# Attention beside scan: decays in SBUF, turned states in two banks, and a new order on four engines

## The chip, the cores and the metric

One core of a Trainium2 chip runs the kernel. The metric is the device time of one execution in microseconds; the time of a kernel is the median of its runs.

## The reference, cut to what matters

Four batches (B = 4) of 512 rows of 512 values pass through two blocks. The first is a selective scan over the context, gated by the normalised rows; the second is causal attention with 16 heads, followed by a mixture of experts.

```python
# first block, for every batch: u is 512 channels x 512 steps, state 512 x 16
dA = exp(delta[..., None] * A)
state = state * dA + (delta * u)[..., None] * B_t
y_t = einsum('ben,bn->be', state, C_t)
...
x = x + tanh(g_xattn) * (y + D * u) * silu(layernorm(x))
# second block
scores = q @ k * HEAD_DIM ** -0.5, causal
ctx = softmax(scores) @ v
h = rms(x + ctx @ wo)
x = x + tanh(g_ffn) * (attention and experts of h)
```

## The kernel before, in words

Everything is float32 (TensorE's large products are split in a high and a low part). Each engine runs its own list of instructions, written out by hand; semaphores are the only link between the lists, and an engine's order is fixed by the order of its calls. Rounds of all engines run as `round_(b, s)` with s = b + 1: the attention of batch b beside the scan of batch s. Ahead of them `first_scan` does batch 0's scan alone, and the fourth round has attention only, with the first pieces of the experts. The experts' part, `moe_stage`, comes last.

In a round, preparations come first (input projection of the context `cT`, convolution, delta, the products for q, k and v). Then `units(b, s)` runs: 16 quads (NQ = 16) of four heads of one block of 128 query rows (T4 = 4 blocks; in block i the scores are 128 x 128(i+1) wide), beside 64 scans (NB = 64: 16 states n times 4 channel blocks et). This is the stage that the change is about; it occurs three times, with s = 1, 2 and 3. Its pieces:

- scan k: ScalarE writes the decay exp(DL * aneg), 128x512, into `decay_bank(s, k)` (line 1269); GpSimd multiplies GB = DU * BB into a ring of four (line 2281, it waits for the scan four before, for its place); VectorE scans both into HS (line 1770), which is a ring of two states n.
- state q: TensorE turns a block of HS into `state_bank(s, q)` (line 705), VectorE adds it, weighted with C, into YA (line 1781).
- attention: TensorE computes the scores of a quad (lines 762 and 765), VectorE the row maxima (line 1826), ScalarE the exponentials EX (`probs`, line 1306), TensorE turns them into the one bank PB (line 775), ScalarE copies them to PT (`keep_turned`, line 1314), TensorE weighs V (`weigh`, lines 786 and 790), ScalarE copies the turned inverse (line 1319), VectorE makes the context cn (line 1836), ScalarE and GpSimd its high and low part (lines 1325 and 2324). VectorE's `invert` (line 1831) and GpSimd's `widen` (line 2318) make the inverse row sums.
- `finish(b, i, step)`: steps of a finished block of rows (output product, residual XL, its gated sum into xa on line 1846, RMS norm, router), spread over the quads of the next block.

SP issues the transfers in its own list: one row of B for each n (`load_b_row`), the rows that finish, and the context of the next batch but one (`load_ctx`). After the stage VectorE ends the scan's output, and TensorE, once the output product of the last rows is done, makes the input projection of the next batch from cT (line 647), on which ScalarE starts the convolution (line 1209).

PSUM has eight banks: A[0] to A[3] hold the scores, CX the context, PB the turned probabilities, HT0 and HT1 are the last two. In the three stages before the change all decays go through HT1 and all turned states but the last three through HT0:

```python
return (A[0], A[2], A[3])[q - (NB - 3)] if q >= NB - 3 else HT0   # state_bank, s > 0
return (HT0, A[0])[q % 2]                                          # state_bank, s == 0
return (HT1, A[1])[k % 2] if s == 0 else HT1                       # decay_bank
if k > (s == 0): act.wait_ge(scan_done, NB * s + k - (s == 0))     # before a decay
if s and 0 < q < NB - 3: pe.wait_ge(y_acc, adds(s, q))             # before a state is turned
```

Elsewhere VectorE has instructions of the same 128x512 with both operands in SBUF: the gate `z_gate` on line 1741 (in the first scan it reads PT and ZS, in later rounds GB and ZS), and the sum into xa on line 1846. Line 1340 is a ScalarE instruction from SBUF to SBUF with a scale for each partition.

## Time and profile before

| | |
|---|---|
| median of 3 runs | 1789.75 us (1787.08 to 1792.86) |
| the profiled execution | 1790.59 us |
| its span in the profile | 1788.8 us |
| TensorE, share of the span | 84% |
| VectorE | 65% |
| ScalarE | 51% |
| GpSimd | 45% |
| mean granted TensorE clock | 0.902 of full speed |
| the three stages, first scan to last | 234.6 to 395.7, 481.7 to 644.8, 730.8 to 890.8 us |

Busy shares are of the whole span, which holds stages of very different kinds: scan, attention beside scan, attention alone, experts. A share says little about any one of them; the rows below are cut by stage where that matters. Times of the profile are microseconds from the start of the span.

### The profile page before, as it was taken

To read this page: it belongs to the slowest core of one execution; us is meant where nothing else is said; L and a number is where in the kernel's file an instruction comes from. 1 tells how busy PE (TensorE), PEld (TensorE's weight loads), DVE (VectorE), ACT (ScalarE), POOL (GpSimd) and SP (SyncE) were. 2 spreads that over 40 slices of the span, in tenths; PEclk is the share of its full clock that TensorE was granted. 3 is DMA by queue.
4 is the path that set the end of the run, shared out by engine and by line. 5 is a ranking of instruction groups with operands and counts; after the bars stand their busy time and mean duration, and the time that the engine had idled before them with its cause. 6 is when DMAs were issued, how large, how long until landed. Compare 5 with 4: busy or idle time off the path is not lost.

```text
span 1788.8 us, 26797 instructions
## 1 busy us (share of the span) xinstructions
PE 1503.7 (84%) x9168; PEld 1150.6 (64%) x9168; DVE 1166.9 (65%) x1699; ACT 916.2 (51%) x2038; POOL 810.2 (45%) x807
## 2 busy tenths in 40 slices
PE   5677967788777789677878998799999999999994
PEld 2344645565445556455655666688787999999973
DVE  5987589996699985899945444432324666566545
ACT  5675457764467753567724663221213666666510
POOL 1992266542466532565413211243422555555444
PEclk8789968899878899788988999899999999999997
DMA  4460001111011111011132004721311877777464
GB/s 168 153 229 19 25 23 55 54 43 54 7 35 55 54 36 31 19 47 54 37 123 95 30 32 160 293 77 59 110 37 65 307 243 253 261 241 253 155 221 165
DMA packets 94664, 195.76 MB, mean 109 GB/s; under 512 B 8945, under 2 KB 25841, under 8 KB 91201
## 3 DMA queue, kind: packets, MB, share of 16 engines
q1 hardware_dynamic: 89408, 177.26, 29.1%
q0 software_dynamic: 5120, 16.78, 2.8%
q8 instruction: 75, 1.23, 0.3%
q14 instruction: 61, 0.49, 0.1%
HBM read 140.40 MB, written 53.61 MB: 108 GB/s over the span
## 4 chain that ended last, share of the span: by engine, by line
PE 55%; DVE 16%; issue 15%; POOL 7%; ACT 5%; DMA 1%; SPq 1%; DVEq 0%; ACTq 0%; POOLq 0%
PE scores L631 21%; PE bank L631 14%; DVE HS L1770 6%; DVE YA L1781 4%; PE bank L705 3%; PE bank L775 3%; POOL GB L2281 2%; PE bank L790 2%; ACT bank L1269 2%; PE bank L825 2%; PE scores L762 2%; POOL yab L2471 2%; PE scores L749 1%; PE bank L1092 1%; PE scores L765 1%
## 5 line engine op out<-in xcount | busy, mean ns | idle before, releaser
L2281 POOL TENSOR_TENSOR GB<-DU,BB 128x512 f32<-128x512 f32 x256 | 326.8, 1298 | 36.1 <-DVE DL L1752 21.2
L1770 DVE TENSOR_TENSOR_SCAN HS<-bank,GB 128x512 f32<-128x512 f32 x224 | 272.0, 1214 | 20.3 <-ACT bank L1269 17.6
L705 PE MATMUL bank<-ident,HS 128*128 128x128 f32 x860 | 165.8, 325 | 120.9 <-DVE YA L1781 104.9
L705 PEld LDWEIGHTS bank<-ident,HS 128*128 128x128 f32 x860 | 115.2, 165 | 166.3 <-DVE YA L1781 129.8
L1269 ACT ACTIVATE bank<-DL,aneg 128x512 f32<-128x512 f32 x224 | 154.7, 691 | 110.0 <-DVE HS L1770 108.2
L775 PE MATMUL bank<-ident,EX 128*128 128x128 f32 x640 | 131.5, 306 | 34.2 <-ACT PT L1314 20.9
L631 PE MATMUL scores<-xth,wgh 128*128 128x256 f32 x552 | 158.1, 286 | 2.2 <-DVE fa L2162 1.3
L1781 DVE SCALAR_TENSOR_TENSOR YA<-bank,Ct,YA 128x512 f32<-128x512 f32 x199 | 147.0, 738 | 14.2 <-PE bank L705 12.8
L631 PE MATMUL scores<-xth,wgl 128*128 128x256 f32 x552 | 156.1, 283 | 0.0
L631 PE MATMUL scores<-xtl,wgh 128*128 128x256 f32 x552 | 156.1, 283 | 0.0
L1314 ACT ACTIVATE PT<-bank 128x128 f32<-128x128 f32 (+3 forms) x256 | 110.3, 431 | 72.0 <-PE bank L775 64.9
L1306 ACT ACTIVATE EX<-scores,nm 128x128 f32<-128x128 f32 (+3 forms) x256 | 132.3, 521 | 22.4 <-DVE nm L1826 21.7
L775 PEld LDWEIGHTS bank<-ident,EX 128*128 128x128 f32 x640 | 79.8, 154 | 75.0 <-issue 47.0
L2426 POOL TENSOR_TENSOR wgl<-wgr,wgh 128x768 fp32r<-128x768 f32 x54 | 110.9, 2057 | 30.4 <-ACT wgh L1580 30.4
L2443 POOL TENSOR_TENSOR fal<-fa,fah 128x512 fp32r<-128x512 f32 x30 | 38.8, 1293 | 162.7 <-ACT fah L1609 162.5
L2324 POOL TENSOR_TENSOR ctl<-cn,cth 128x128 fp32r<-128x128 f32 x64 | 29.3, 458 | 180.7 <-ACT cth L1325 180.7
L631 PEld LDWEIGHTS scores<-xth,wgh 128*128 128x128 f32 x552 | 105.7, 191 | 3.6 <-DVE fa L2162 1.7
L631 PE MATMUL scores<-hah,wgh 128*128 128x512 f32 x272 | 106.7, 392 | 1.0 <-issue 1.0
L631 PE MATMUL scores<-hal,wgh 128*128 128x512 f32 x272 | 106.5, 391 | 0.0
L631 PE MATMUL scores<-hah,wgl 128*128 128x512 f32 x272 | 106.3, 391 | 0.0
L631 PEld LDWEIGHTS scores<-xtl,wgh 128*128 128x128 f32 x552 | 105.7, 192 | 0.9
L631 PEld LDWEIGHTS scores<-xth,wgl 128*128 128x128 f32 x552 | 105.7, 191 | 0.0
(294 smaller groups left out, 3798.6 us busy)
## 6 DMA issues: line engine op xcount, KB each, us to landing
wgr<-wffn_in SPq DMA_DIRECT2D x108, 384.0 KB, 6.5
wdr<-wffn_in SPq DMA_DIRECT2D x81, 256.0 KB, 3.1
BB<-b_scratch SPq DMA_DIRECT2D x64, 256.0 KB, 3.3
xr<-xg SPq DMA_DIRECT2D x23, 512.0 KB, 5.8
yg<-ysb SPq DMA_DIRECT2D x23, 512.0 KB, 6.5
xg<-V SPq DMA_DIRECT2D x11, 1024.0 KB, 5.8
hah<-hhd SPq DMA_DIRECT2D x5, 1024.0 KB, 14.1
hal<-hhd SPq DMA_DIRECT2D x5, 1024.0 KB, 16.1
```

Source lines behind the costliest of these rows:

```text
L631: mm = nc.tensor.matmul(out_, parts[a](k), rhs_parts[b](k), start=(k == 0 and j == 0), stop=(k == n - 1 and j == 2))
L705: mm = nc.tensor.transpose(state_bank(s, q)[:, et * P:(et + 1) * P], HS[:, n % 2, et, tt * P:(tt + 1) * P], ident[:])
L762: nc.tensor.matmul(SB[:, a, 0:W], QK[r:r + HD, m, i * P:(i + 1) * P], QK[r:r + HD, 4 + m, 0:W], start=True, stop=False)
L775: mm = nc.tensor.transpose(turned_bank(b, v)[:, kb * P:(kb + 1) * P], EX[:, a, kb * P:(kb + 1) * P], ident[:])
L1269: nc.scalar.activation(decay_bank(s, k), DL[:, et, :], ACT.Exp, scale=aneg[:, et, n:n + 1]).then_inc(dA_ready, 1)
L1306: nc.scalar.activation(EX[:, a, 0:W], SB[:, a, 0:W], ACT.Exp, bias=nm[:, a:a + 1], accum_out=rs[:, q % 2, a:a + 1]).then_inc(ex_done, 1)
L1314: nc.scalar.activation(PT[:, a, 0:W], turned_bank(b, v)[:, 0:W], ACT.Copy).then_inc(pt_done, 1)
L1770: nc.vector.tensor_tensor_scan(HS[:, n % 2, et, :], decay_bank(s, k), GB[:, k % 4, :], 0.0, ALU.mult, ALU.add).then_inc(scan_done, 1)
L1781: nc.vector.scalar_tensor_tensor(YA[:, tt, :], state_bank(s, q), Ct[:, tt, n:n + 1], YA[:, tt, :], ALU.mult, ALU.add).then_inc(y_acc, 1)
L2281: nc.gpsimd.tensor_tensor(GB[:, k % 4, :], DU[:, et, :], BB[:, n % 2, :], ALU.mult).then_inc(gb_ready, 1)
L2426: nc.gpsimd.tensor_tensor(wgl[raw][:, c, :], wgr[raw][:, c * 2 * EW:(c + 1) * 2 * EW], wgh[raw][:, c, :].bitcast(f32), ALU.subtract).then_ ...
L2443: nc.gpsimd.tensor_tensor(fal[:, b % 2, c, :], fa[:, s % 2, :], fah[:, b % 2, c, :].bitcast(f32), ALU.subtract).then_inc(f_al, 1)
```

## The change

Decays of the three stages move from the PSUM bank HT1 to two halves of cT, the context's place in SBUF, which lies idle once the input projection has read it. A decay waits for the scan two before, not one. Turned states use HT0 and HT1 in turn, and one is turned once the state two before has been added. As the decays now lie in cT, the next context is loaded after the stage's last scan and not ahead of the stage. The order of the instructions in `units` is written anew on TensorE, ScalarE, VectorE and GpSimd; the instructions themselves, their sizes and their number stay as they are.

```diff
@@ -380,7 +380,7 @@
 
             if s == 0:
                 return (HT0, A[0])[q % 2]
-            return (A[0], A[2], A[3])[q - (NB - 3)] if q >= NB - 3 else HT0
+            return (A[0], A[2], A[3])[q - (NB - 3)] if q >= NB - 3 else HT[q % 2]
 
         def z_bank(s, tt):
 
@@ -406,7 +406,8 @@
             return VT * NS + NB * (s - 1) + q
 
         def decay_bank(s, k):
-            return (HT1, A[1])[k % 2] if s == 0 else HT1
+
+            return cT[:, k % 2, :] if s else (HT1, A[1])[k % 2]
 
         def turned_bank(b, v):
 
@@ -430,6 +431,8 @@
         def _(sp):
             def load_ctx(s):
                 at(sp, xp_mm, T4 * s)
+                if s > 1:
+                    sp.wait_ge(scan_done, NB * s)
                 sp.dma_start(cT[:], ctx_in[s]).then_inc(ctx_in_s, 16)
 
             def load_x(s, i):
@@ -502,8 +505,6 @@
                 if s < B:
                     sp.wait_ge(xd_ready, s + 1)
                     sp.dma_start(b_scratch[s], xd[DR:DR + NS, :]).then_inc(b_stored, 16)
-                    if 0 < s < B - 1:
-                        load_ctx(s + 1)
                     sp.wait_ge(b_stored, 16 * (s + 1))
                     for n in range(2):
                         load_b_row(s, n)
@@ -537,6 +538,8 @@
                     i, m = quad(q)
                     if b >= 0 and i and m:
                         rows_out(b, i - 1, m - 1)
+                if 0 < s < B - 1:
+                    load_ctx(s + 1)
 
             begin()
             for r in range(-1, B):
@@ -699,8 +702,8 @@
                         pe.wait_ge(y_acc, adds(0, q - 1))
                     else:
                         pe.wait_ge(kept, 2 * weighed(m, ut) + 2)
-                if s and 0 < q < NB - 3:
-                    pe.wait_ge(y_acc, adds(s, q))
+                if s and 1 < q < NB - 3:
+                    pe.wait_ge(y_acc, adds(s, q - 1))
                 for et in range(T4):
                     mm = nc.tensor.transpose(state_bank(s, q)[:, et * P:(et + 1) * P],
                                              HS[:, n % 2, et, tt * P:(tt + 1) * P], ident[:])
@@ -887,20 +890,14 @@
                 for q in range(-2, NQ + 1):
                     now, next_, last = 0 <= q < NQ, 0 <= q + 1 < NQ, 0 < q
                     i, m = quad(q)
-                    row = i - 1 if now and i else None
-                    if now:
-                        turn(b, HG * q + 1)
-                    if last:
-                        turn_states(s, T4 * (q - 1) + 1)
                     if now:
                         turn(b, HG * q + 2)
-                    if row is not None and m != 1:
-                        finish(b, row, (0, None, 1, 2)[m])
-                    if last:
-                        turn_states(s, T4 * (q - 1) + 2)
+                    if now and i and m != 1:
+                        finish(b, i - 1, (0, None, 1, 2)[m])
                     if now:
                         turn(b, HG * q + 3)
                     if last:
+                        turn_states(s, T4 * (q - 1) + 2)
                         turn_states(s, T4 * (q - 1) + 3)
                     if now:
                         weigh(b, q)
@@ -910,6 +907,10 @@
                         turn_states(s, T4 * q)
                     if q + 2 < NQ:
                         scores(b, q + 2)
+                    if next_:
+                        turn(b, HG * (q + 1) + 1)
+                    if now:
+                        turn_states(s, T4 * q + 1)
 
 
             def last_units(b):
@@ -1264,8 +1265,8 @@
                     act.wait_ge(dt_rel, T4 * s + T4)
                 if n == 0:
                     act.wait_ge(dl_s, T4 * s + et + 1)
-                if k > (s == 0):
-                    act.wait_ge(scan_done, NB * s + k - (s == 0))
+                if k > 1:
+                    act.wait_ge(scan_done, NB * s + k - 1)
                 nc.scalar.activation(decay_bank(s, k), DL[:, et, :], ACT.Exp, scale=aneg[:, et, n:n + 1]
                                      ).then_inc(dA_ready, 1)
 
@@ -1369,43 +1370,39 @@
 
 
             def units(b, s):
-                decay(s, 1)
-                for q in range(-1, NQ + 1):
-                    now, next_ = 0 <= q < NQ, q + 1 < NQ
+                for q in range(-2, NQ):
+                    now, next_ = 0 <= q, 0 <= q + 1 < NQ
                     i, m = quad(q)
-                    row = i - 1 if now and i else None
-                    v, w, k = HG * q, HG * (q + 1), T4 * q
-                    if now:
-                        keep_turned(b, v + 2)
-                    if next_:
-                        probs(b, w)
-                        probs(b, w + 1)
-                    if now:
-                        decay(s, k + 3)
-                        keep_turned(b, v + 3)
+                    row, below = i - 1 if now and i else None, quad(q + 1)
+                    w, k, x = HG * (q + 1), T4 * (q + 1), HG * (q + 2)
+                    if next_ and k:
+                        decay(s, k)
                     if next_:
                         probs(b, w + 2)
-                    if row is not None and m in (0, 2):
-                        finish(b, row, m + 1)
-                    if 0 < q + 1 < NQ:
-                        decay(s, k + 4)
-                    if next_:
                         probs(b, w + 3)
                     if now:
                         keep_inverse(b, q)
                     if next_:
+                        decay(s, k + 1)
                         keep_turned(b, w)
-                    if now and next_:
-                        decay(s, k + 5)
+                        decay(s, k + 2)
                     if row is not None and m == 1:
                         finish(b, row, 2)
                     if now:
                         context(b, q)
+                    if row is not None and m == 0:
+                        finish(b, row, 1)
                     if next_:
                         keep_turned(b, w + 1)
-                        decay(s, k + 6)
-                    if now and m == 3 and i + 1 < T4:
-                        finish(b, i, 0)
+                        decay(s, k + 3)
+                        keep_turned(b, w + 2)
+                    if q + 2 < NQ:
+                        probs(b, x)
+                        probs(b, x + 1)
+                    if next_ and below[0] and below[1] in (0, 2):
+                        finish(b, below[0] - 1, (0, None, 3)[below[1]])
+                    if next_:
+                        keep_turned(b, w + 3)
 
 
             def last_units(b):
@@ -1889,39 +1886,37 @@
 
 
             def units(b, s):
-                scan(s, 0)
-                row_max(b, 0)
-                scan(s, 1)
-                for q in range(-1, NQ + 1):
+                for q in range(-2, NQ + 1):
                     now, next_, last = 0 <= q < NQ, 0 <= q + 1 < NQ, 0 < q
                     i, m = quad(q)
-                    row = i - 1 if now and i else None
+                    row, below = i - 1 if now and i else None, quad(q + 1)
                     k = T4 * q
                     if row is not None and m == 3:
                         finish(b, row, 3)
+                    if now:
+                        scan(s, k + 3)
                     if row is not None and m == 0:
                         finish(b, row, 1)
                     if last:
                         add_state(s, k - 2)
-                    if row is not None and m == 2:
-                        finish(b, row, 2)
-                    if now:
-                        scan(s, k + 3)
+                    if next_:
+                        scan(s, k + 4)
                     if last:
                         add_state(s, k - 1)
-                    if now and next_:
-                        scan(s, k + 4)
+                    if next_:
+                        invert(b, q + 1)
                     if now:
                         context(b, q)
+                    if next_:
+                        scan(s, k + 5)
+                    if now:
                         add_state(s, k)
-                    if next_:
-                        invert(b, q + 1)
-                    if now and next_:
-                        scan(s, k + 5)
                     if q + 2 < NQ:
                         row_max(b, q + 2)
                     if now:
                         add_state(s, k + 1)
+                    if next_ and below[0] and below[1] == 2:
+                        finish(b, below[0] - 1, 2)
                     if next_:
                         scan(s, k + 6)
 
@@ -2349,27 +2344,23 @@
 
 
             def units(b, s):
-                driven(s, 1)
-                driven(s, 2)
-                for q in range(0, NQ + 1):
-                    now = 0 <= q < NQ
-                    i, m = quad(q)
+                for q in range(0, NQ + 2):
+                    now, last = q < NQ, 0 < q <= NQ
+                    i, m = quad(q - 1)
                     k = T4 * q
-                    if q > 0:
+                    if last and i and m in (1, 3):
+                        finish(b, i - 1, m // 2)
+                    if q > 1:
+                        context(b, q - 2)
+                    if now and q:
+                        driven(s, k)
+                    if now:
+                        driven(s, k + 1)
+                    if last:
                         widen(b, q - 1)
-                    if now and i and m == 3:
-                        finish(b, i - 1, 1)
-                    if now and q:
-                        driven(s, k + 1)
+                    if now:
                         driven(s, k + 2)
-                    if q > 0:
-                        context(b, q - 1)
-                    if now:
                         driven(s, k + 3)
-                    if now and i and m == 1:
-                        finish(b, i - 1, 0)
-                    if q + 1 < NQ:
-                        driven(s, k + 4)
 
 
             def last_units(b):
```

## Rows read from the trace of the kernel before

Times are microseconds, durations marked as means or in groups are ns. PE is TensorE, PEld its weight load, DVE VectorE, ACT ScalarE, POOL GpSimd. The row of a stretch gives its length, then the busy us of PE, PEld, DVE, ACT and POOL with their instructions, the granted clock, the DMA share and GB/s. That of a group gives busy us, mean ns and the idle time before it with what ended it.

**Rows 1.** The page: busy us, share of the span, instructions; busy tenths in 40 slices.

```profile
PE 1503.7 (84%) x9168; PEld 1150.6 (64%) x9168; DVE 1166.9 (65%) x1699; ACT 916.2 (51%) x2038; POOL 810.2 (45%) x807
...
DVE  5987589996699985899945444432324666566545
```

**Rows 2.** Busy time by stretch, each from a stage's first scan to its last.

```profile
234.60:395.70 161.10, 121.86 (x988) 86.17 (x992) 148.68 (x184) 114.55 (x300) 95.89 (x105) 0.81 0.17 48
481.70:644.80 163.10, 123.94 (x988) 87.78 (x992) 148.03 (x184) 114.50 (x300) 95.86 (x105) 0.80 0.16 48
730.80:890.80 160.00, 119.82 (x992) 83.98 (x996) 147.74 (x184) 114.08 (x300) 95.89 (x105) 0.82 0.14 44
```

**Rows 3.** VectorE's groups, first stage: busy us, mean ns | idle before, releaser.

```profile
L1770 DVE TENSOR_TENSOR_SCAN HS<-bank,GB 128x512 f32<-128x512 f32 x64 | 77.8, 1215 | 6.4 <-ACT bank L1269 5.9 <-POOL GB L2281 0.2
L1781 DVE SCALAR_TENSOR_TENSOR YA<-bank,Ct,YA 128x512 f32<-128x512 f32 x61 | 45.1, 739 | 3.8 <-PE bank L705 3.6
L1826 DVE TENSOR_REDUCE nm<-scores 128x4 f32<-128x512 f32 (+3 forms) x16 | 23.5, 1468 | 1.5 <-PE scores L765 1.5
L1836 DVE TENSOR_TENSOR cn<-bank,rbs 128x128 f32<-128x128 f32 x16 | 4.3, 271 | 0.5 <-ACT rbs L1319 0.3
```

**Rows 4.** VectorE's waits in the second and third stage: us, times, longest.

```profile
DVE HS L1770 <- ACT bank L1269: 5.6, 20, 0.9
DVE YA L1781 <- PE bank L705: 4.7, 7, 1.2
...
DVE HS L1770 <- ACT bank L1269: 6.0, 22, 0.9
DVE YA L1781 <- PE bank L705: 2.4, 5, 1.2
```

**Rows 5.** ScalarE: the decays of the first stage; line 1340, ns min/median/max.

```profile
L1269 ACT ACTIVATE bank<-DL,aneg 128x512 f32<-128x512 f32 x63 | 43.5, 691 | 34.8 <-DVE HS L1770 34.4
...
L1340 ACT ACTIVATE hp<-XL,r x16: 706/712/736, 293.4 to 1097.6; 128x512 f32<-128x512 f32 x16
```

**Rows 6.** The scan's line in the third stage: duration ns min/median/max.

```profile
L1770 DVE TENSOR_TENSOR_SCAN HS<-bank,GB x64: 1190/1214/1225, 730.8 to 889.5; 128x512 f32<-128x512 f32 x64
```

**Rows 7.** Line 1741, ns min/median/max; VectorE, then GpSimd in order of time: start, duration.

```profile
L1741 DVE SCALAR_TENSOR_TENSOR ZS<-GB,ZS x12: 683/689/694, 195.9 to 692.5; 128x512 f32<-128x512 f32 x12
L1741 DVE SCALAR_TENSOR_TENSOR ZS<-PT,ZS x4: 860/1373/2753, 54.3 to 76.9; 128x512 f32<-128x512 f32 x4
...
54.27 2.75 DVE L1741 SCALAR_TENSOR_TENSOR ZS<-PT,ZS 128x512 f32<-128x512 f32 x1
...
52.70 3.78 POOL L2281 TENSOR_TENSOR GB<-DU,BB 128x512 f32<-128x512 f32 x3
55.14 1.34 POOL L2281 TENSOR_TENSOR GB<-DU,BB 128x512 f32<-128x512 f32 x1
```

**Rows 8.** The sum into xa in the three stages: duration ns min/median/max.

```profile
L1846 DVE SCALAR_TENSOR_TENSOR xa<-XL,tg,xa x3: 752/1307/1795, 278.0 to 363.4; 128x512 f32<-128x512 f32 x3
...
L1846 DVE SCALAR_TENSOR_TENSOR xa<-XL,tg,xa x3: 752/753/1209, 526.1 to 610.7; 128x512 f32<-128x512 f32 x3
...
L1846 DVE SCALAR_TENSOR_TENSOR xa<-XL,tg,xa x3: 750/752/1159, 775.2 to 858.5; 128x512 f32<-128x512 f32 x3
```

**Rows 9.** GpSimd's low part of the context and widening, first stage.

```profile
L2324 POOL TENSOR_TENSOR ctl<-cn,cth 128x128 fp32r<-128x128 f32 x15 | 6.9, 457 | 50.0 <-ACT cth L1325 50.0
L2318 POOL TENSOR_TENSOR rib<-ri,one 128x128 f32<-128x128 f32 x16 | 6.5, 406 | 0.1
```

**Rows 10.** The first stage's last scan, the next projection, the context's transfer.

```profile
394.43 1.22 DVE L1770 TENSOR_TENSOR_SCAN HS<-bank,GB 128x512 f32<-128x512 f32 x1
395.56 0.73 DVE L1781 SCALAR_TENSOR_TENSOR YA<-bank,Ct,YA 128x512 f32<-128x512 f32 x1
...
402.73 0.59 PE L647 MATMUL bank<-cT,w_in 128*128 128x512 f32 x1
...
DMA to landing us min/median/max: 3.5/4.1/5.6
```

## The prediction

> **What bounds the kernel now.** The page's busy shares name no single bound: TensorE leads with 84% of the span, but VectorE, 65% on average, has digits of 8 and 9 in most slices of the first half and of 2 to 6 later [rows 1]. So the span has to be cut. The change touches only the three stages in which attention of batch b runs beside the scan of batch b+1, so I cut there, from the first scan to the last: 161.1, 163.1 and 160.0 us [rows 2]. In them VectorE is busy for 148.7, 148.0 and 147.7 us, TensorE for 120 to 124, ScalarE for 114 and GpSimd for 96. VectorE is what each stage lasts by; all that could be had by a better order is what it stands idle, 12.4 + 15.1 + 12.3 = 39.8 us. Its work in one stage is 64 scans of 1.22 us, 64 additions of a turned state of 0.74 us, and 16 row maxima of 1.47 us on average [rows 3]. The waits say what the idle time is made of [rows 3, 4]: the scan waits for ScalarE's decay, 5.9 + 5.6 + 6.0 = 17.5 us in the three stages, and the addition waits for TensorE's turned state, 3.6 + 4.7 + 2.4 = 10.7 us. The rest, 11.6 us, is in the stage's start (two row maxima wait 1.5 us for scores in the first), in row steps and in gaps too short to be put down to anyone. These two waits are what rings of two are about: with a single bank a decay can't be written before the scan that reads the last one has ended, and a state can't be turned before the last one is added.
>
> **The change, part by part.**
>
> Decays in a ring of two. ScalarE may write decay k once scan k-2 is done, so the 17.5 us of waits can go. In return the decay lies in SBUF and not in PSUM. For ScalarE that is 0.69 against 0.71 us of its nearest SBUF-to-SBUF instruction with a scale per partition [rows 5], 64 times 0.02 = 1.3 us a stage on an engine with 46 us idle [rows 2]: nothing. If it should become a cost, it would show as a longer wait of the scan for the decay.
>
> For VectorE the move is what decides. A scan so far reads one operand from PSUM and one (GB) from SBUF, and its 64 durations in the third stage lie between 1.19 and 1.23 us, whatever GpSimd does [rows 6]. After the change both operands are in SBUF. The trace has no scan of this size with two, but it has additions and products of the same 128x512 with two. With GpSimd idle such a one takes 0.69 us (12 times, 0.683 to 0.694); the same product, run while GpSimd multiplies, takes 0.86 to 2.75 us in its four cases; with twice the median they make 6.36 us, a mean of 1.59 [rows 7]. The timeline shows why: one that starts at 54.27 ends at 57.02, that is 0.54 us after GpSimd's third product in a row has ended (55.14 + 1.34 = 56.48). It stood still through the rest of one product and through a whole further one. So two such instructions exclude each other: one waits until the other is done. Whether the scan joins them no row of before shows; its own rows, all with one SBUF operand, would leave the sum at the waits won, -27 us (below). The Trainium skill makes no exception for the scan (SBUF — State Buffer, "Who interferes with whom"): a VectorE instruction with two SBUF inputs takes its second through the read interface that GpSimd has, and whichever comes first holds it for its whole length. By that rule the sum could not be under the floor of +20 us that is worked out below. For products and additions the trace agrees, with the 56.48 and 57.02 above.
>
> The price by which one scan gets longer. Lower bound: 0, if scans were spared; no gain either, since the addition of a state, with one operand in PSUM, takes 0.74 us, and the like operation with two in SBUF 0.75 [rows 3, 8]. Near bound: in the very stages of the change the gated sum into xa has two SBUF operands; it comes three times in each, and the nine durations sum to 9.23 us [rows 8]. Five of them are 0.75, where nothing is in its way: (9.23 - 6.75) / 9 = 0.28 us. Upper bound: 1.59 - 0.69 = 0.90 us [rows 7]. Between them I walk through one period of the new order. An instruction of VectorE starts some 0.08 us before the last one ends [rows 10], so a scan counts 1.13 us, an addition 0.66, a maximum 1.39; a product of GpSimd 1.25 (3.78 for three [rows 7]). Two scans now stand back to back, so GpSimd is held off for both and then has two products due. An addition (0.66) covers half of the first: the third scan waits 0.6 us, or 1.8 if GpSimd's second product follows without a break as at 55.14. After it an addition, the context (0.27 - 0.08) [rows 3] and a reciprocal of four values (under 0.1) are 0.9 us and stand against 1.25: 0.3 us. After the fourth scan come addition, maximum, addition, 2.7 us, against two products and the two small operations of 0.46 and 0.41 us [rows 9], 3.4: 0.7 us. Together 1.6 to 2.8 us a period, 0.40 to 0.70 us a scan. I take **0.40**, the walk's low end, since the row nearest to it, of these very stages, gives 0.28: 64 x 0.40 = 25.6 us a stage, 76.8 us in three.
>
> **A floor.** GpSimd is busy 95.9 us a stage, all of it reading SBUF [rows 2, 9]. If scans and its work exclude each other, no stage can be shorter than 64 x 1.13 + 95.9 = 168.2 us, 7.1, 5.1 and 8.2 us above today's: 20.4 us lost in all, and a time of 1811 us or more, unless the ends of the instructions overlap.
>
> Turned states in two banks, HT0 and HT1. TensorE turns state q while state q-1 is being added: the 10.7 us can go. No instruction is added, and TensorE has 39 us idle a stage.
>
> The new order. The same instructions on each engine. GpSimd's low part of the context moves one step back, so that it no longer stands waiting for ScalarE (50.0 us in one stage [rows 9]) in front of products; its products then come sooner after each scan, which is also when the next scan wants the operands. At the start the second decay stands behind four exponentials; the second scan comes about 0.4 us later than now (three times: 1.2 us). I count the waits won as 28.2 - 1.2 = **27 us**.
>
> The context's load. It moves from before the attention to after the last scan, on SP, for batches 2 and 3. It lands in 3.5 to 5.6 us; today the last scan ends at 395.65 and the input projection that reads it starts at 402.73, 7.1 us later, while TensorE is at its output product [rows 10]. Cost: nothing, at worst (5.6 and an issue of 0.4, on a stage end shortened by 1 or 2 us) 1 us each. Behind it on SP stand the stores of the last finished row, whose sum needs that output product too, so it is no earlier than the projection, and then the next rows of B, which need the convolution that follows it.
>
> **Sum.** 76.8 - 27 = +50 us. The profiled execution took 1790.6 us (a span of 1788.8); 1790.6 + 50 = 1840.6. The median of the runs shown is 0.8 us lower, so the forecast is **1840 us**.
>
> **Rivals.**
> (1) The scan is spared, and the change does what its rings allow: 1790.6 - 27 = 1764 us; if every idle gap went, 1751. For it: no row shows a scan hindered. Against it: every other two-operand instruction of this size is.
> (2) No stage moves much. The waits won and the collisions cancel, which takes 27 / 192 = 0.14 us a scan, half the low bound; or the scan is spared and new waits take the won ones' place, as ScalarE now puts decay, exponentials and copies of turned blocks in one queue with only two decays ahead. Either gives 1786 to 1795.
> (3) GpSimd keeps hold through runs of products, as at 55.14, in most periods: 0.90 us a scan, 172.8 - 27 = +146, 1936 us. Against it: in steady state a product may start only when the scan four before it is done, so runs are short.
> Mechanism and turning point are one for all: what a scan loses to GpSimd. Under 0.14 us the change is faster, above it slower.
>
> **Chances.** Forecast (0.25 to 0.65 us a scan, 1790.6 - 27 + 192 times that, 1812 to 1888) 0.66, rival 1 0.20, rival 2 0.08, rival 3 0.06. What a measurement of this kernel can tell from no change is about 0.3%, 5 us. So faster 0.21 (rival 1 and an edge of 2), same 0.07, slower 0.72. The likeliest case's own range is 1812 to 1888; the whole reaches down into rival 1 and up to 0.65 us a scan: **1766 to 1888**, with rival 3 and the faster half of rival 1 left out.
>
> **What would show it.** Right: scans whose durations spread from 1.2 up to 2.5 us where all were 1.2, mean near 1.6; GpSimd's products longer too, up to 2.4 us; the scan's waits for the decay nearly gone; stages of 175 to 182 us; the rest of the span as before. Wrong: scans all at 1.2 us, stages of 150 to 153 us. If the scan's waits for GpSimd's product grow instead, GpSimd is the later one. If scans are at 1.2 and the stages at 161, look for the idle time before additions and reciprocals. If ScalarE's first step of the next convolution waits for a projection that starts over 8 us after the last scan, the context's load was late.

## The result, and the profile after

The changed kernel takes 1798.45 us (median of 6 runs, 1797.32 to 1800.55) against 1788.8 us before on the same chips: a ratio of 1.0054, 95% interval 1.0041 to 1.0066. It is slower by about 10 us. The forecast was 50 us slower (1840 us), with 1812 to 1888 for its likeliest case and 1766 to 1888 for the whole. The time lies inside the whole range, but below the likeliest case and above rival (1); rival (2), 1786 to 1795 with a chance of 0.08, came nearest. The sign and the mechanism were right, the size was not.

First the page of the changed kernel (busy us, share, instructions; then the costliest groups, busy us and mean ns, idle time before them):

```profile
PE 1511.5 (84%) x9168; PEld 1156.5 (64%) x9168; DVE 1208.6 (67%) x1699; ACT 916.2 (51%) x2038; POOL 946.1 (53%) x807
...
L2276 POOL TENSOR_TENSOR GB<-DU,BB 128x512 f32<-128x512 f32 x256 | 409.7, 1632 | 49.1 <-DVE HS L1767 27.7
L1767 DVE TENSOR_TENSOR_SCAN HS<-cT,GB 128x512 f32<-128x512 f32 x192 | 282.1, 1487 | 2.7 <-ACT cT L1270 1.5 <-POOL GB L2276 1.2
...
L1778 DVE SCALAR_TENSOR_TENSOR YA<-bank,Ct,YA 128x512 f32<-128x512 f32 x199 | 143.9, 725 | 1.8 <-PE bank L708 1.7
```

Compared with [rows 1] VectorE is busy for 41.7 us more and GpSimd for 135.9 us more, with not one instruction added. A busy time that grows while the count stays the same means that instructions got longer, or stood still while they counted as busy. The scan did: 1.487 us on average instead of 1.215, 192 times. Then the three stages, first scan to last, as in [rows 2]:

```profile
235.30:397.80 162.50, 126.15 (x968) 88.83 (x968) 160.83 (x182) 114.42 (x300) 140.46 (x105) 0.76 0.15 46
484.80:647.20 162.40, 122.25 (x968) 86.08 (x968) 160.87 (x182) 114.29 (x300) 140.59 (x105) 0.80 0.15 46
734.20:896.70 162.50, 122.06 (x968) 86.19 (x968) 160.96 (x182) 114.39 (x300) 140.68 (x105) 0.80 0.13 43
```

The lengths add to 487.4 us; before they were 161.1 + 163.1 + 160.0 = 484.2 [rows 2]. VectorE's idle time is 1.67 + 1.53 + 1.54 = 4.7 us where it was 39.8: hardly any waiting is left to win. But its busy time is 482.7 us where it was 444.5. So 35 us of waiting were won and 38 us of busy time were paid, +3.2 us. The scans by themselves got 192 x 0.272 = 52 us longer; VectorE's other busy time in the stages fell by 14 us. About 4 of these 14 us only moved out of the stretch (three additions now follow a last scan, three row maxima come ahead of a first one). The rest of the span's +7.8 us lies around the stages: 0.7 us ahead of the first, 1.0 us behind the first and behind the second (a moved addition and a moved row maximum lie between two stages), 1.9 us behind the third.

What remains of VectorE's waits in the first stage, which before were those of [rows 3]:

```profile
DVE HS L1767 <- ACT cT L1270: 0.5, 1, 0.5
DVE cn L1833 <- ACT rbs L1320: 0.4, 1, 0.4
DVE HS L1767 <- POOL GB L2276: 0.4, 1, 0.4
DVE lg L1853 <- PE bank L634: 0.2, 1, 0.2
```

Of the two waits that the rings are about, 5.9 and 3.6 us in this stage before, 0.5 us is left of the first and nothing of the second. And how the price is paid can be read instruction by instruction. VectorE first, then GpSimd, start and duration:

```profile
322.24 1.19 DVE L1767 TENSOR_TENSOR_SCAN HS<-cT,GB 128x512 f32<-128x512 f32 x1
325.64 1.65 DVE L1767 TENSOR_TENSOR_SCAN HS<-cT,GB 128x512 f32<-128x512 f32 x1
332.21 2.09 DVE L1767 TENSOR_TENSOR_SCAN HS<-cT,GB 128x512 f32<-128x512 f32 x1
334.23 1.35 DVE L1767 TENSOR_TENSOR_SCAN HS<-cT,GB 128x512 f32<-128x512 f32 x1
...
322.40 2.12 POOL L2276 TENSOR_TENSOR GB<-DU,BB 128x512 f32<-128x512 f32 x1 [1.16 <-DVE HS L1767]
...
324.46 1.75 POOL L2276 TENSOR_TENSOR GB<-DU,BB 128x512 f32<-128x512 f32 x1
...
331.93 1.30 POOL L2276 TENSOR_TENSOR GB<-DU,BB 128x512 f32<-128x512 f32 x1
...
333.17 1.33 POOL L2313 TENSOR_TENSOR rib<-ri,one 128x128 f32<-128x128 f32 x1
334.46 2.19 POOL L2276 TENSOR_TENSOR GB<-DU,BB 128x512 f32<-128x512 f32 x1
```

The scan of 322.24 ends at 323.43; the product that was issued at 322.40 ends at 324.52, 1.09 us later, though one alone takes 1.28. The product of 324.46 ends at 326.21; the scan issued at 325.64 ends at 327.29, 1.08 us later. The product of 331.93 ends at 333.23, the scan of 332.21 at 334.30, 1.07 us later; and then the widening `rib`, 0.41 us by itself, ends at 334.50, 0.20 us after that scan, and so on to the scan of 334.23 (ends 335.58) and the product behind it (336.65, again 1.07 us). They take turns, one each, and each turn costs about 1.08 us for a scan or a product, not the 1.2 or 1.3 us of the whole instruction. This holds beyond these rows: 84 of the 192 scans last over 1.4 us, exactly one GpSimd instruction ends within each of them, and the scan ends 1.075 to 1.086 us after it.

### The profile page after: what moved, and what is told of

Read it like the earlier page. It is cut to its first block, busy times and chain, and to the rows that moved or that the text cites. A ratio compares the mean times of both kernels' runs of the same rounds, so it can differ in the third digit from the quotient of the medians.

```text
span 1796.6 us, 26796 instructions
## 1 busy us (share of the span) xinstructions
PE 1511.5 (84%) x9168; PEld 1156.5 (64%) x9168; DVE 1208.6 (67%) x1699; ACT 916.2 (51%) x2038; POOL 946.1 (53%) x807
## 4 chain that ended last, share of the span: by engine, by line
PE 51%; issue 16%; DVE 16%; POOL 12%; ACT 4%; DMA 1%; SPq 1%; DVEq 0%; ACTq 0%; POOLq 0%
PE scores L634 21%; PE bank L634 14%; POOL GB L2276 6%; DVE HS L1767 5%; DVE YA L1778 4%; PE bank L708 2%; PE bank L778 2%; PE bank L828 2%; POOL yab L2462 2%; PE bank L793 2%; PE scores L765 1%; PE scores L752 1%; PE bank L1093 1%; POOL h2l L2334 1%; DVE nm L1823 1%
## 5 line engine op out<-in xcount | busy, mean ns | idle before, releaser
L2276 POOL TENSOR_TENSOR GB<-DU,BB 128x512 f32<-128x512 f32 x256 | 409.7, 1632 | 49.1 <-DVE HS L1767 27.7
L1767 DVE TENSOR_TENSOR_SCAN HS<-cT,GB 128x512 f32<-128x512 f32 x192 | 282.1, 1487 | 2.7 <-ACT cT L1270 1.5
L708 PE MATMUL bank<-ident,HS 128*128 128x128 f32 x860 | 160.4, 325 | 45.0 <-DVE YA L1778 29.0
L708 PEld LDWEIGHTS bank<-ident,HS 128*128 128x128 f32 x860 | 120.3, 168 | 77.0 <-DVE YA L1778 33.6
L1270 ACT ACTIVATE cT<-DL,aneg 128x512 f32<-128x512 f32 x192 | 138.3, 720 | 52.0 <-DVE HS L1767 50.8
L634 PE MATMUL scores<-xth,wgl 128*128 128x256 f32 x552 | 156.1, 283 | 0.0
L634 PE MATMUL scores<-xtl,wgh 128*128 128x256 f32 x552 | 156.1, 283 | 0.0
L2434 POOL TENSOR_TENSOR fal<-fa,fah 128x512 fp32r<-128x512 f32 x30 | 38.8, 1292 | 162.7 <-ACT fah L1606 162.5
L2123 DVE SCALAR_TENSOR_TENSOR ft<-ft,scores 128x512 f32<-128x512 f32 x30 | 20.6, 687 | 119.1 <-ACT ft L1599 119.1
```

The lines of the kernel that those rows point to most:

```text
L634: mm = nc.tensor.matmul(out_, parts[a](k), rhs_parts[b](k), start=(k == 0 and j == 0), stop=(k == n - 1 and j == 2))
L708: mm = nc.tensor.transpose(state_bank(s, q)[:, et * P:(et + 1) * P], HS[:, n % 2, et, tt * P:(tt + 1) * P], ident[:])
L1270: nc.scalar.activation(decay_bank(s, k), DL[:, et, :], ACT.Exp, scale=aneg[:, et, n:n + 1]).then_inc(dA_ready, 1)
L1767: nc.vector.tensor_tensor_scan(HS[:, n % 2, et, :], decay_bank(s, k), GB[:, k % 4, :], 0.0, ALU.mult, ALU.add).then_inc(scan_done, 1)
L2276: nc.gpsimd.tensor_tensor(GB[:, k % 4, :], DU[:, et, :], BB[:, n % 2, :], ALU.mult).then_inc(gb_ready, 1)
L2434: nc.gpsimd.tensor_tensor(fal[:, b % 2, c, :], fa[:, s % 2, :], fah[:, b % 2, c, :].bitcast(f32), ALU.subtract).then_inc(f_al, 1)
```

## The experiments

Times are medians; "before" is the kernel before, run on the same chip. The changed kernel's 1798.45 us is from the chips of the result; beside the experiments the kernel before took 1788.5 to 1789.0 us.

**1. The operand's place alone.** The kernel before, with this edit and the late load of the context:

```diff
-            return (HT1, A[1])[k % 2] if s == 0 else HT1
+            return (HT1, A[1])[k % 2] if s == 0 else cT[:, 0, :]
```

> The order of before, one state bank, one decay at a time, but each decay lies in the first half of cT and the next context is loaded after the last scan. If the operand's place alone costs what the scan gained in length after the change (1.487 - 1.215 = 0.27 us), and nothing absorbs it, 192 scans give +52 us: 1835 to 1850, scans with a mean of 1.45 to 1.55 us, waits for decays as before (17 us) or longer. Rival: the longer scans only fill idle time that the stage has anyway; then under 1810.

Measured: 1849.05 us against 1788.47, ratio 1.034 (1.0322 to 1.0357), +60.6 us. Scans and the waits in front of them, all three stages (ns min/median/max; us and times):

```profile
L1772 DVE TENSOR_TENSOR_SCAN HS<-cT,GB x192: 1192/1307/2312, 238.6 to 948.9; 128x512 f32<-128x512 f32 x192
...
  ACT cT L1271: 21.4, 70
```

The mean of the three stages is 1.471, 1.474 and 1.489 us, so 192 x 0.263 = 50 us of scans, and the waits for a decay grew from 17.5 to 21.4 us. Nothing absorbs the price. The rival falls. A likely reason why the waits grew is that a decay, which must wait for the scan before it, comes later when that scan is longer; no run separates this.

**2. The rings, in the old order.** The kernel before with the change's edits for decays, states, waits and load, and none of the four new orders.

```diff
-            return (A[0], A[2], A[3])[q - (NB - 3)] if q >= NB - 3 else HT0
+            return (A[0], A[2], A[3])[q - (NB - 3)] if q >= NB - 3 else HT[q % 2]
...
-            return (HT1, A[1])[k % 2] if s == 0 else HT1
+            return cT[:, k % 2, :] if s else (HT1, A[1])[k % 2]
```

> Both rings of two (decays in cT, states in HT0 and HT1) and the late load, in the order of before. If the rings win the waits, this is as fast as the changed kernel, 1795 to 1803, with VectorE idle under 3 us a stage. Rival: the waits go by the new order; then VectorE keeps 8 us or more of idle time a stage and the time is 1815 to 1840.

Measured: 1829.25 us, ratio 1.023 (1.0213 to 1.0247). The first stage of it:

```profile
236.20:410.60 174.40, 123.63 (x1000) 87.50 (x1000) 170.05 (x184) 113.81 (x300) 135.53 (x105) 0.80 0.15 45
```

Neither theory had this right. The time is that of the rival (1815 to 1840), the idle time that of neither: 4.4 us in this stage and 13.0 us in all three, of 39.8 before. So the rings by themselves win most of the waits, and the kernel is 20 us faster than that of the first experiment. What is dear here is the scan, 1.59 us on average. The new order, 31 us faster than this, does two things: it takes the idle time from 13.0 to 4.7 us, and it makes collisions cheaper, 1.487 us a scan against 1.59, which is 20 us.

**3. The new order, one bank each.** The changed kernel, with decays through HT1 and states through HT0 and the waits of before.

```diff
-            return cT[:, k % 2, :] if s else (HT1, A[1])[k % 2]
+            return HT1 if s else (HT1, A[1])[k % 2]
...
-                if s and 1 < q < NB - 3:
-                    pe.wait_ge(y_acc, adds(s, q - 1))
+                if s and 0 < q < NB - 3:
+                    pe.wait_ge(y_acc, adds(s, q))
```

> The new order and the late load, with one decay at a time in PSUM (HT1) and one state bank (HT0), as before. Scans are at 1.21 us in either theory. If the order alone can win the waits: 1755 to 1770. If it needs the rings (decays and states come in pairs, back to back): idle time of 15 us a stage or more, 1789 to 1830.

Measured: 1942.38 us, ratio 1.0859 (1.0841 to 1.0877), outside both ranges on the side of the second. VectorE's waits in the first stage:

```profile
DVE HS L1767 <- ACT bank L1270: 17.6, 27, 0.9
DVE HS L1767 <- PE bank L708: 16.7, 14, 1.2
DVE YA L1778 <- PE bank L708: 9.7, 14, 1.4
DVE nm L1823 <- PE scores L768: 6.7, 11, 1.2
```

Scans are at 1.22 us, but 57 of the stage's 206.9 us are idle. With one bank each the new order is 154 us slower than the old one; the fifth experiment gives it one of the two rings back.

**4. No reads by GpSimd.** The changed kernel; in the three stages GpSimd writes GB with zeros, so batches 1 to 3 are scanned with an input of zero.

```diff
-                nc.gpsimd.tensor_tensor(GB[:, k % 4, :], DU[:, et, :], BB[:, n % 2, :], ALU.mult).then_inc(gb_ready, 1)
+                if s:
+                    nc.gpsimd.memset(GB[:, k % 4, 0:L // 2], 0.0)
+                    nc.gpsimd.memset(GB[:, k % 4, L // 2:L], 0.0).then_inc(gb_ready, 1)
+                else:
+                    ...
```

> The changed kernel, but in the three stages GpSimd writes zeros into GB (two halves) and reads nothing, so that batches 1 to 3 are scanned with an input of zero. If the scans are long because they and GpSimd's products exclude each other at a read of SBUF, they fall back to 1.21 us, the stages to 148 to 152 us and the time to 1752 to 1765. Rival: a scan with both operands in SBUF is slower by itself; then the mean stays near 1.49 us and the time near 1798.

Measured: 1736.33 us, ratio 0.9713 (0.9697 to 0.973). The scans (ns min/median/max), then the first and second stage:

```profile
L1767 DVE TENSOR_TENSOR_SCAN HS<-cT,GB x192: 1189/1210/1358, 235.4 to 835.7; 128x512 f32<-128x512 f32 x192
```

```profile
235.40:378.90 143.50, 111.75 (x968) 78.98 (x968) 142.38 (x182) 112.83 (x300) 60.22 (x163) 0.88 0.18 54
463.30:608.20 144.90, 116.17 (x984) 83.47 (x988) 142.96 (x182) 113.33 (x300) 59.66 (x163) 0.85 0.17 53
```

A scan with both operands in SBUF is no slower by itself: the median is 1.21 us and the mean 1.218, against 1.215 before. The whole surplus comes with GpSimd's reads. The stages came out shorter than I had expected, 143.5 to 144.9 and not 148 to 152. This kernel splits the result in two steps: with two zero writes (0.31 us each) in place of a product, rings and order come out 1788.5 - 1736.3 = 52 us faster than the kernel before; putting the products back costs 1798.4 - 1736.3 = 62 us. The sum is the +10. The split is not clean. The zero writes also leave GpSimd 60 us of work a stage instead of 96 [rows 2] and spare the sums into xa their collisions, and the kernel before was not run with zero writes, so how much of the 52 us rings and order are worth by themselves is not shown.

**5. One state bank under the new order.** The changed kernel with the third experiment's edit of the states alone.

```diff
-            return (A[0], A[2], A[3])[q - (NB - 3)] if q >= NB - 3 else HT[q % 2]
+            return (A[0], A[2], A[3])[q - (NB - 3)] if q >= NB - 3 else HT0
...
-                    pe.wait_ge(y_acc, adds(s, q - 1))
+                    pe.wait_ge(y_acc, adds(s, q))
```

> The changed kernel, decays in a ring of two, but all turned states through HT0, each turned once the last one is added. If the new order lives from two states at a time (TensorE turns two back to back, and VectorE adds one before and one after a scan or a maximum): 1815 to 1880, with the additions waiting for TensorE. Rival: the decays' ring is what the order needs, the states' isn't: under 1805.

Measured: 1885.06 us, ratio 1.0522 (1.0495 to 1.0548). In the first stage the scan waits 14.7 us for TensorE, which must have turned the old states out of HS before the scan may write there:

```profile
DVE HS L1767 <- PE bank L708: 14.7, 14, 1.2
DVE nm L1823 <- PE scores L768: 9.7, 11, 1.3
DVE YA L1778 <- PE bank L708: 2.0, 3, 0.8
```

The rival is refuted: the new order does need the states' ring. But the expectation had the place wrong, and its range (1815 to 1880) ended 5 us short: the additions wait only 2.0 us, the scans and the row maxima wait 24.4. One state bank costs the changed kernel 86.6 us. Against the third experiment the decays' ring brings 57 us, so under the new order both rings are needed.

**6. The late load alone.** The kernel before with the moved load of the next context, nothing else.

```diff
+                if s > 1:
+                    sp.wait_ge(scan_done, NB * s)
                 sp.dma_start(cT[:], ctx_in[s]).then_inc(ctx_in_s, 16)
...
-                    if 0 < s < B - 1:
-                        load_ctx(s + 1)
...
+                if 0 < s < B - 1:
+                    load_ctx(s + 1)
```

> The kernel before, with the load of the next context moved behind the stage's last scan and nothing else. If the load is hidden behind TensorE's output product: no change, ratio 1.000, first projections 7.1 us after the last scan. Rival: it is late by 1 us each time or more, which gives 2 us or more in two stages, a ratio of 1.001 to 1.003.

Measured: 1787.15 us against 1788.84, ratio 0.9994 (0.9985 to 1.0003). It costs nothing that can be measured. In the changed kernel the projection starts at 405.20, 7.4 us after the last scan's end.

**7. GpSimd's old order.** The changed kernel, GpSimd's `units` as before, the other three engines' new.

```diff
+                driven(s, 1)
+                driven(s, 2)
...
-                        driven(s, k)
...
-                    if last:
-                        widen(b, q - 1)
...
+                    if q + 1 < NQ:
+                        driven(s, k + 4)
```

> The changed kernel, with GpSimd's order of before and the other three engines' new one. The scan's mean was 1.59 us in the old order of all engines and 1.487 in the new. If GpSimd's place of its products is what makes collisions dear or cheap: a mean near 1.59 and 1798 + 192 x 0.1 = 1817, 1808 to 1825. Rival: VectorE's order sets it, GpSimd only follows the scans; then 1798 to 1803 and a mean of 1.49 to 1.51.

Measured: 1810.34 us, ratio 1.0117 (1.0093 to 1.0141). VectorE's first stage is busy 164.16 of 164.80 us:

```profile
235.90:400.70 164.80, 125.13 (x968) 88.87 (x968) 164.16 (x182) 114.83 (x300) 139.28 (x105) 0.77 0.16 47
```

and its scans in all three stages:

```profile
L1767 DVE TENSOR_TENSOR_SCAN HS<-cT,GB x192: 1194/1352/2244, 235.9 to 902.0; 128x512 f32<-128x512 f32 x192
```

The time lies in the first theory's range, the scan's length between the two: 1.59 us over the first 28 of a stage and 1.49 to 1.51 over the rest, 1.54 in all. So GpSimd's order makes about half of the difference between 1.59 and 1.487, and that of the other engines the rest. The stages are 2.3 to 2.4 us longer each, 7 us in all, and that is also what this profiled execution (1805.26 us) took more than the changed kernel's (1798.38). The other three executions took 1809.76 to 1811.17; where these 5 us come from no trace shows.

**8. A price by the piece.** Zeros for the scans 0 to 27 of a stage only, products for the rest (the first 28 blocks are scanned with an input of zero).

```diff
-                if s:
+                if s and k < 28:
```

> The changed kernel, with zeros written by GpSimd into GB in place of the products for the scans 0 to 27 of each stage (so these blocks are scanned with an input of zero). It says what it is worth that 28 scans and their products are apart, with nothing else moved: 27 us if the price is the same all through the stage, 1768 to 1776. Rival: the price is paid mostly in the later quads, where GpSimd and ScalarE are busier; then 1780 or more.

Measured: 1768.49 us, ratio 0.9885 (0.987 to 0.99), 30 us under the changed kernel. That is the first theory's 27 us and a little more. The lengths of the changed kernel's scans agree: 1.57 us on average over the first 28 of a stage and 1.42 over the other 36, against 1.215 before. So the price is paid all through the stage, and per scan it is higher at the start. The next experiment looks for a way to spare these 28 scans the collision with GpSimd's products left in.

**9. Free banks for 28 decays, three times.** Scores of the first eight quads are at most 256 wide, and two heads fit in one bank. That frees A[2] and A[3] for the decays 0 to 27, which then lie in PSUM again; states keep HT0 and HT1. A stage's first decay now also waits until these banks are free of v; its first scan begins 1 to 2 us later (236.2 to 237.4 us in the first stage of the three kernels, against 235.3).

```diff
+            if s and k < K1:
+                return A[2 + k % 2]
             return cT[:, k % 2, :] if s else (HT1, A[1])[k % 2]
+        def head(q, a):
+            W = P * (quad(q)[0] + 1)
+            if q < 8:
+                return SB[:, a // 2, a % 2 * 2 * P:a % 2 * 2 * P + W]
+            return SB[:, a, 0:W]
```

TensorE makes the scores of heads 0 and 2, waits for them by a semaphore, and makes those of 1 and 3:

```diff
-                for a in range(HG):
...
+                for first in ((0, 1), (2, 3)) if q >= 8 else ((0, 2), (1, 3)):
+                    for a in first:
...
+                    if q < 8 and first[0] == 0:
+                        mm.then_inc(rt_split, 1)
+                        pe.wait_ge(rt_split, 8 * b + q + 3)
```

> The changed kernel, but for the first eight quads of a stage, whose scores are at most 256 wide, the scores of two heads share a bank, and the decays 0 to 27 go through the two banks that this frees, in PSUM; from decay 28 on they lie in cT. TensorE makes the scores of these quads in two steps with a wait of its own between. If what the change costs is the exclusion of scans with two SBUF operands, 28 of 64 scans are spared it: 28/64 of the 62 us that the kernel without GpSimd's reads gained on the changed one, 27 us, so 1766 to 1778, faster than the kernel before as well, with those scans at 1.21 us. Rival: the two steps of the scores delay the row maxima and with them everything; then 1785 to 1800.

Measured: 1802.91 us, ratio 1.0077 (1.0059 to 1.0095). The expectation fell. The stages were 157.8, 158.2 and 156.1 us, 15 us less than the changed kernel's in all and not 27. Part of that is the rival's reason: VectorE is idle for 18.5 us of them where it was 4.7, and in the first stage its largest wait is that of the row maxima.

```profile
DVE nm L1844 <- PE scores L784: 4.3, 4, 2.5
```

The larger part lies elsewhere: from the third stage's last scan to the end it took 919 us instead of 900. The two-step scores also stood in the last attention, beside which no scan runs. So, with the two steps only where a scan runs:

```diff
+        def packed(b, q):
+            return b < B - 1 and q < 8
...
-            if q < 8:
+            if packed(b, q):
```

> As the kernel with the freed banks, but the two-step scores only where a scan runs beside (the fourth batch's attention, which runs alone, keeps its four banks). In the last run the three stages were 15 us shorter in all than the changed kernel's and the part behind them 19 us longer. If that part is longer because the two steps stand bare in the attention without a scan: 1803 - 19 = 1784, 1780 to 1787, a little under the kernel before. Rival: the later part suffers from something else that the freed banks bring; then over 1795.

Measured: 1799.98 us, ratio 1.0058 (1.0039 to 1.0078): the rival's range. The stages were a little shorter still (156.0, 156.1, 155.0), the end was again 919 us. My edit had left the heads of the wide scores in pairs, too: heads 0 and 1, their masks, heads 2 and 3, their masks. The next kernel puts them back to four heads and then four masks, and in the stages makes the first half of the scores ahead of a turning of states, the second behind it:

```diff
+                    if 0 <= q < 6:
+                        scores(b, q + 2, 0)
                     if now:
                         turn_states(s, T4 * q)
                     if q + 2 < NQ:
-                        scores(b, q + 2)
+                        scores(b, q + 2, 1 if 0 <= q < 6 else None)
```

> The same, with the first half of the scores made before the turning of a state and the second behind it, so that TensorE need not stand for its own result. The first 28 scans of a stage then take 61 us, against 58 where GpSimd reads nothing; if the scores are what holds them, 1 to 2 us a stage come back: 1776 to 1783. Rival: it makes the additions late instead; then as the run before or up to 5 us above.

Measured: 1778.46 us, ratio 0.9934 (0.9915 to 0.9954). This kernel is faster than both: 10.6 us under the one before, 20 us under the changed one. The time lies in the expected range, but by luck: the range is the 1780 to 1787 expected of the last kernel, which did not come, less the 1 to 2 us a stage, and the expectation did not name the return to four heads. TensorE's scores in the attention alone, 960 to 1060 us, first with pairs of heads, then with four:

```profile
L784 PE MATMUL scores<-QK 32*128 32x256 f32 (+3 forms) x96 | 20.4, 502 | 0.0
```

```profile
L791 PE MATMUL scores<-QK 32*128 32x256 f32 (+3 forms) x96 | 11.1, 536 | 0.0
```

The same 96 products of 32 rows take 20.4 us of TensorE in pairs and 11.1 us in fours, although a single one lasts about as long (0.50 and 0.54 us): their records overlap, on average 2.4 at a time in pairs (96 x 0.502 / 20.4) and 4.6 in fours. Over the whole part behind the stages TensorE is busy 19 us less, and that part is 18 us shorter. The edit changes the size of the groups and the place of the masks together; which of the two counts is not shown. In the stages 2 us were won (154.6, 155.5, 154.9); the wide scores went back to four heads there too, so these 2 us can't be put down to the halves alone. The scans of this kernel, in both places:

```profile
L1797 DVE TENSOR_TENSOR_SCAN HS<-cT,GB x108: 1191/1334/2087, 298.3 to 875.3; 128x512 f32<-128x512 f32 x108
L1797 DVE TENSOR_TENSOR_SCAN HS<-scores,GB x84: 1192/1212/1224, 237.4 to 781.1; 128x512 f32<-128x512 f32 x84
```

Within one run, with GpSimd's products beside both groups, the scans with the decay in PSUM last 1.19 to 1.22 us; those with it in SBUF go up to 2.09.

## Why the prediction was right or wrong, point by point

*That VectorE bounds the stages:* right. It is busy for 99% of them after the change, TensorE for 76% (370.5 of 487.4 us).

*That the scan joins the exclusion:* right; the fourth experiment and the last one's two groups show it. The rule of the Trainium skill (SBUF — State Buffer, "Who interferes with whom") holds for the scan: with two SBUF operands it contends with a GpSimd instruction that reads SBUF (mean 1.487 us) and not with one that only writes it (1.218 us).

*Its price, 0.40 us a scan:* too high, and the main step that failed. It measured 0.272 us, 52 us and not 76.8. The row nearest to it, the sum into xa at 0.28 us [rows 8], had it; the walk through a period, which I set above the row, did not. The walk counted a product as 1.25 us that holds a scan off for all of it; the trace shows turns of 1.08 us, and no long scan with two products ahead of it. By the scan's place in the period the walk charged at least 0.6 us to the one behind the pair and its addition, 0.3 to the one behind the context, 0.7 to the first of the next pair and nothing to the second, 1.6 us a period. The scans of the three stages are longer by 0.40, 0.17, 0.34 and 0.18 us at these places, 1.09 us. So the three charged places cost little more than half of what the walk gave them, and the uncharged one has a price too.

*The floor of 168.2 us a stage:* broken, 162.5 us. It was built on whole instructions, as is the rule of the same section of the Trainium skill as the prediction took it. The trace does not agree in this: the second instruction ends about 1.08 us after the first, which is less than its own 1.21 or 1.28 us, and here the measurement decides. With 1.08 us a turn, scans and products need 64 x 2 x 1.08 = 138 us, and the small operations fit in. The prediction's "unless the ends of the instructions overlap" is what happened.

*The waits won, 27 us:* too low, the other failed step. I summed only the waits that the profile puts down to a releaser, 28.2 us, and left 11.6 us to "gaps too short". Of the 39.8 us of idle time 35.1 went. And I took the idle time for the most that could be had, but VectorE's busy time apart from the longer scans fell too, by 14 us. About 4 us of that is work moved out of the stretch. About 6 us is hand-over: where VectorE does not stand idle, an instruction starts some 0.08 us before the last one ends, and its gaps in the three stages fell from 131 to 25, so the instructions overlap more. The last 4 us are additions a little shorter on average (0.724 us, 0.739 before) and small operations; why, no run shows. So a closed gap was worth its own length and some 0.06 us more. The fourth experiment agrees: there the busy time fell from 444.5 to 428.3 us, 2.5 us of it in the sums into xa, which collide no more.

The errors pulled the same way. By the profiles, the sum of +50 was to be 76.8 - 27; it was 52 for the scans, -35 for the idle time, -14 for VectorE's other busy time and +5 around the stages, +8. The price is off by 25 us, the idle time by 8, and the other two, which the prediction put at nothing, by 9 together: that is the 42 us between. The sign hung on the difference of two terms of about 50 us each; a range of 0.25 to 0.65 us with the gain held fixed at 27 did not show how close they were.

*The turned states at 10.7 us:* far too low as a part of the change. With one state bank the new order loses 86.6 us. That the wait of before was small because the old order was built around it is my reading; no run shows it.

*The context's load:* right, nothing.

*Rivals:* (1), the scan spared, is refuted. (2) named nearly the right outcome, waits and price close to cancelling, but put the turning point at 0.14 us. With the 35 us of idle time, the 14 us of other busy time and the 5 us lost around the stages it is (35 + 14 - 5) / 192 = 0.23 us, a little under the measured price of 0.27. (3) is refuted: within each of the 84 scans over 1.4 us just one GpSimd instruction ends.

*Signs to look for:* scans from 1.19 to 2.29 us, products up to 2.2 us, the decay's wait gone: as forecast. The mean near 1.6 us and the stages of 175 to 182 us did not come: they are 1.487 and 162.5 us.

## What to carry to other kernels

When an operand moves from PSUM to SBUF, look for GpSimd beside it: the scan with two SBUF operands paid by collisions with GpSimd's products here, 0.27 us on top of 1.2, and the best guide to that price was a like instruction in the same stage. A new order and new buffers are one change: the order here costs 154 us without the rings, the rings in the old order are 31 us slower than with the new one, and a wait that is small under one order says nothing about what the buffer is worth under another. Sum what an engine is idle, not only the waits with a name, and give the gain a range of its own.

## What the runs showed of the hardware that was not expected

The scan and GpSimd's product exclude each other for about 1.08 us, less than either lasts (1.21 and 1.28 us), and in the three stages they take turns even where GpSimd works without a break (331.93 to 336.65); in the kernel before one product of VectorE had been held off through two of GpSimd's [rows 7]. The small `rib` on GpSimd, 0.41 us by itself, counted 1.04 us on average and its group 16.6 us of the first stage instead of 6.5 [rows 9], with the same sixteen instructions; the turn at 333.17 above shows such a wait:

```profile
L2313 POOL TENSOR_TENSOR rib<-ri,one 128x128 f32<-128x128 f32 x16 | 16.6, 1035 | 0.0
L2319 POOL TENSOR_TENSOR ctl<-cn,cth 128x128 fp32r<-128x128 f32 x15 | 11.5, 768 | 3.2 <-ACT cth L1326 3.2
```

And the order in which TensorE's products of 32 rows for four heads and their masks are issued was worth 18 us in the part behind the stages.
